# The last stage of a fused attention and mixture-of-experts kernel: the dense part written into PSUM by ScalarE, a fifth place for results, an earlier exponential and earlier stores

## The reference

```python
xn = layernorm(x) * ln_gamma + ln_beta
abel_out = gelu(xn @ abel_w + abel_b)                 # the dense (shared) part
topw, topi = top_k(xn @ moe_gate_w + moe_gate_b, 2)   # two experts per row
w_dense = one_hot(topi) weighted with softmax(topw)
eo = gelu(xn @ ew1[e] + eb1[e]) @ ew2[e] + eb2[e]
moe_out = sum over the two chosen e of w_dense[e] * eo   # then three rotations
gate = sigmoid(concat(abel_out, moe_out) @ gc_w + gc_b)
mixed = abel_out * (1 - gate) + moe_out * gate
return residual + mixed
```

## Time and profile before

| | |
|---|---|
| median of three runs | 1321.17 us |
| the profiled execution | 1317.45 us, span 1315.8 us |
| PE busy in the span | 1175.7 us (89%) |
| DVE busy | 863.6 us (66%) |
| ACT busy | 494.9 us (38%) |
| POOL busy | 417.5 us (32%) |
| mean granted clock of TensorE | 0.935 |
| last expert tile out of PSUM (line 1461) | ends at 1274.80 us |

### The profile page before, as it was taken

The page is one execution under the profiler, slowest core; times in us unless marked ns, Lnnn a source line. Parts: engine busy times, 40 slices in busy tenths (PEclk is TensorE's granted clock), DMA queues, the critical chain, the costliest instruction groups (busy, mean ns, idle before and its releaser), DMA issues.

```text
span 1315.8 us, 25930 instructions
## 1 busy us (share of the span) xinstructions
PE 1175.7 (89%) x7208; PEld 1017.0 (77%) x7209; DVE 863.6 (66%) x2771; ACT 494.9 (38%) x961; POOL 417.5 (32%) x496
## 2 busy tenths in 40 slices
PE   6989969886999999967999989999776999999988
PEld 6746657675888898956889878888664888988977
DVE  7669767745666666677776677676544766666666
ACT  1115624342444344432333333343333344444445
POOL 3003016862444444430000000114562344444430
PEclk9999968777999999988999989999867999999999
DMA  9402324444444533351101110001226633443358
GB/s 297 140 8 97 128 80 153 159 147 157 122 137 136 168 88 95 91 190 49 49 3 47 49 49 1 1 13 53 97 92 235 197 123 122 132 147 107 104 187 284
DMA packets 72688, 149.15 MB, mean 113 GB/s; under 512 B 10950, under 2 KB 36754, under 8 KB 72602
## 3 DMA queue, kind: packets, MB, share of 16 engines
q1 hardware_dynamic: 52234, 93.40, 20.3%
q0 software_dynamic: 19584, 53.92, 13.4%
q10 hardware_dynamic: 784, 0.79, 0.2%
HBM read 82.63 MB, written 65.44 MB: 113 GB/s over the span
## 4 chain that ended last, share of the span: by engine, by line
PE 51%; issue 11%; DVE 6%; POOL 5%; DMA 4%; another core or an unknown queue 3%; ACT 3%; SPq 2%; POOLq 1%; DVEq 0%; ACTq 0%
PE bank L2450 17%; PE bank L1986 7%; PE bank L1987 6%; PE bank L1988 6%; PE bank L2015 3%; DMA xh<-slots_in 3%; PE bank L2068 3%; PE bank L1846 2%; PE bank L2508 2%; POOL slots_in L1562 2%; PE bank L1998 2%; POOL xh L1573 2%; POOLq L1572 1%; PE bank L2461 1%
## 5 line engine op out<-in xcount | busy, mean ns | idle before, releaser
L1986 PE MATMUL bank<-ew,rows 128*128 x852 | 298.9, 351 | 7.4 <-DVE rows L1440 5.2
L1987 PE MATMUL bank<-low_in,rows 128*128 x852 | 274.2, 322 | 0.0
L1988 PE MATMUL bank<-ew,rows 128*128 x852 | 272.8, 320 | 0.0
L1585 POOL DMA_INDIRECT results<-xh x142 | 142.0, 1000 | 292.6 <-DVE xh L1468 272.0
L1986 PEld LDWEIGHTS bank<-ew,rows 128*128 128x128 f32 x852 | 162.0, 190 | 19.0 <-issue 11.8
L1988 PEld LDWEIGHTS bank<-ew,rows 128*128 128x128 f32 x852 | 161.5, 190 | 11.7
L1813 ACT ACTIVATE xh<-bank 128x512 f32<-128x512 f32 x142 | 85.1, 599 | 222.7 <-PE bank L1988 222.7
L1987 PEld LDWEIGHTS bank<-low_in,rows 128*128 128x128 f32 x852 | 162.4, 191 | 6.2
L1477 DVE TENSOR_TENSOR rows<-bank,rows 128x512 fp32r<-128x512 f32 x142 | 98.2, 691 | 95.1 <-ACT rows L202 86.2
L735 POOL TENSOR_TENSOR work<-work,mhalf 128x8 f32<-128x8 f32 x24 | 40.0, 1666 | 298.4 <-DVE work L728 286.1
L1846 PE MATMUL bank<-abw,work 128*128 128x8 f32 (+1 forms) x512 | 113.3, 370 | 18.7 <-ACT work L207 9.3
(11 more groups left out here) (371 smaller groups left out, 2037.1 us busy)
## 6 DMA issues: line engine op xcount, KB each, us to landing
xh<-slots_in POOLq DMA_DIRECT2D x138, 129.0 KB
low_in<-low SPq DMA_DIRECT2D x32, 512.0 KB
ew<-results SPq DMA_DIRECT2D x7, 1032.0 KB, 9.1
xh<-results SPq DMA_DIRECT2D x6, 1032.0 KB, 5.3
dense<-ab SPq DMA_DIRECT2D x12, 512.0 KB
xs<-in_L_attn_a_x_dram SPq DMA_DIRECT2D x4, 1024.0 KB, 8.0
ew<-in_L_ffn_ew_dram SPq DMA_DIRECT2D x2, 2048.0 KB, 13.2
ew<-in_L_ffn_ew_dram SPq DMA_DIRECT2D x4, 1024.0 KB, 14.6
```

The source lines that it names most:

```text
L1585: pool.indirect_dma_start(out=yg, out_offset=bass.IndirectOffsetOnAxis(ap=back[j % RING], axis=0), in_=yr[j % RING], in_offset=None).then_ ...
L1986: pe.matmul(o, hi, f32r(high(c)), start=(c == 0), stop=False)
L1987: pe.matmul(o, hi, f32r(low(c)), start=False, stop=False)
L1988: last = pe.matmul(o, lo, f32r(high(c)), start=False, stop=(stop and c == chunks[-1]))
```

## The change

Four things, all in the last stage of `mixture(1)`:

- The dense part's product leaves TensorE. ScalarE writes share times dense tile, 256 columns, into the PSUM place (`mixed`), and TensorE adds two products to what is there (`start=False`). So that TensorE adds and does not overwrite, it first writes all eight banks once with a matmul that starts a sum (eight of 512 columns, bf16, after the last expert tile); ScalarE waits for these before its first copy. Diagonals are now 6 a group, and the wait for a free bank moves from TensorE to ScalarE.
- Results get a fifth place, in the tile `rows`. Group 4 is loaded right behind `returned(3)`; group g from 5 on waits for group g - 5.
- ScalarE issues the exponential of group g + 1 inside group g, behind the copy of the third tile and ahead of that tile's two diagonals.
- SyncE stores group 0 before it refills for group 7, and the store of group 7 is two halves.

```diff
-            dg = [dg.take(3 * BYP, P) for _ in range(2)]
+            dg = [dg.take(2 * BYP, P) for _ in range(2)]
...
-                        ] + [ew1[:].rearrange("p a e h -> p a (e h)")[:, :, 0:2 * 2 * CW]]
+                        ] + [ew1[:].rearrange("p a e h -> p a (e h)")[:, :, 0:2 * 2 * CW],
+                             rows[:].rearrange("p a b n -> p (a b n)")[:, 0:GT * 2 * CW].rearrange("p (t x) -> p t x", x=2 * CW)]
+            PLACES = len(res_flat)
+            res_place = lambda g: g if g < PLACES else g - PLACES
...
+            def mixed(g, t):
+                return bank[:, 2 * (g % RING) + t // HALF, t % HALF * C:(t % HALF + 1) * C]
+
+            def dense_row(g, t):
+                return ab[:, g * GT + t, :]
...
                 returned(LOWS - 1)
+                if r == 1:
+                    results_in(RING)
...
-                for g in range(RING, NG) if r == 1 else ():
-                    sp.wait_ge(mix_ps, 2 * (g - RING + 1))
-                    sp.wait_ge(last_ok, 3 * (g - RING + 1))
-                    results_in(g)
...
+                    def refill(g):
+                        sp.wait_ge(mix_ps, 2 * (g - PLACES + 1))
+                        sp.wait_ge(last_ok, 3 * (g - PLACES + 1))
+                        results_in(g)
+
+                    def store(some):
+                        sp.dma_start(o[:, some, :], xs[:, some, :]).then_inc(o_st, 16)
+
+                    for g in range(PLACES, NG - 1):
+                        refill(g)
                     for g in range(NG):
+                        if g == NG - 1:
+                            sp.wait_ge(x2_ok, 2 * g + 1)
+                            store(slice(g * GT, g * GT + HALF))
                         sp.wait_ge(x2_ok, 2 * (g + 1))
                         sp.wait_ge(last_ok, 3 * (g + 1))
-                        sp.dma_start(o[:, tiles(g), :], xs[:, tiles(g), :]).then_inc(o_st, 16)
-                    sp.wait_ge(o_st, 16 * NG)
+                        store(tiles(g) if g < NG - 1 else slice(g * GT + HALF, (g + 1) * GT))
+                        if g == 0:
+                            refill(NG - 1)
+                    sp.wait_ge(o_st, 16 * (NG + 1))
...
-                for g in range(NG) if r == 1 else ():
+
+                def raise_gate(g):
                     act.wait_ge(z_ok, g + 1)
                     act.activation(z[g % 2], z[g % 2], ACT.Exp, scale=-1.0).then_inc(ez_ok, 1)
+
+                if r == 1:
+                    raise_gate(0)
+                for g in range(NG) if r == 1 else ():
                     act.wait_ge(gate_ok, 2 * (g + 1))
                     for t in range(BYP):
                         after(act, mix_ps, 2 * (g - 2) + t // HALF + 1)
-                        parts = (gw2[g % 2][:, t, 0:1], gw2[g % 2][:, t, 1:2], shut[g % 2][:, t:t + 1])
-                        for k, part in enumerate(parts):
-                            last = copy(act, dg[g % 2][:, 3 * t + k, :], ident[:], part)
+                        if g == 0 and t == 0:
+                            act.wait_ge(dn_ps, out_past + SLOTS + 1)
+                        if t % HALF == 0:
+                            after(act, x2_ok, 2 * (g - RING) + t // HALF + 1)
+                        copy(act, mixed(g, t), dense_row(g, t), shut[g % 2][:, t:t + 1])
+                        if t == BYP - 1 and g + 1 < NG:
+                            raise_gate(g + 1)
+                        for k in range(2):
+                            last = copy(act, dg[g % 2][:, 2 * t + k, :], ident[:], gw2[g % 2][:, t, k:k + 1])
                         if t % HALF == HALF - 1 or t == BYP - 1:
                             last.then_inc(dg_ok, 1)
...
+                if r == 1:
+
+
+                    pe.wait_ge(y_ok, past + SLOTS)
+                    for b in range(2 * RING):
+                        last = pe.matmul(bank[:, b, :], onesb[0:2 * QROW + E, :], sel[:, 0:BANK // P, :].rearrange("p e c -> p (e c)"),
+                                         start=True, stop=True)
+                    last.then_inc(dn_ps, 1)
...
                         if t % HALF == 0:
                             pe.wait_ge(dg_ok, 2 * g + t // HALF + 1)
-                            after(pe, x2_ok, 2 * (g - RING) + t // HALF + 1)
-                        o = bank[:, 2 * (g % RING) + t // HALF, t % HALF * C:(t % HALF + 1) * C]
-                        src = (result_row(g, t, 0), result_row(g, t, 1), ab[:, g * GT + t, :])
-                        for k in range(3):
-                            last = pe.matmul(o, dg[g % 2][:, 3 * t + k, :], src[k], start=(k == 0), stop=(k == 2))
+                        for k in range(2):
+                            last = pe.matmul(mixed(g, t), dg[g % 2][:, 2 * t + k, :], result_row(g, t, k), start=False, stop=(k == 1),
+                                             skip_group_check=True)
```

More of the change, by code:

```diff
@@ L1089, in mixture @@
             BYP = GT - 1
-            dg = Arena(work[:, T - 2 * 3 * BYP * P:T])
-            assert rt.at <= T - 2 * 3 * BYP * P
-            dg = [dg.take(3 * BYP, P) for _ in range(2)]
+            dg = Arena(work[:, T - 2 * 2 * BYP * P:T])
+            assert rt.at <= T - 2 * 2 * BYP * P
+            dg = [dg.take(2 * BYP, P) for _ in range(2)]
             ntile, tincl, ends = rt.take(E), rt.take(E), rt.take(E)
@@ L1128, in mixture @@
             res_flat = [ew2[:].rearrange("p a e c -> p a (e c)")[:, :, q * 2 * CW:(q + 1) * 2 * CW] for q in range(RING - 1)
-                        ] + [ew1[:].rearrange("p a e h -> p a (e h)")[:, :, 0:2 * 2 * CW]]
+                        ] + [ew1[:].rearrange("p a e h -> p a (e h)")[:, :, 0:2 * 2 * CW],
+                             rows[:].rearrange("p a b n -> p (a b n)")[:, 0:GT * 2 * CW].rearrange("p (t x) -> p t x", x=2 * CW)]
+            PLACES = len(res_flat)
+            res_place = lambda g: g if g < PLACES else g - PLACES
             res = [v.rearrange("p a (t k c) -> p a t k c", k=2, c=CW) for v in res_flat]
+            def mixed(g, t):
+                return bank[:, 2 * (g % RING) + t // HALF, t % HALF * C:(t % HALF + 1) * C]
+            def dense_row(g, t):
+                return ab[:, g * GT + t, :]
             def result_row(g, t, k):
-                v = res[g % RING]
+                v = res[res_place(g)]
                 return v[:, t // v.shape[2], t % v.shape[2], k, 0:C]
@@ L1176, in mixture @@
             if r == 1:
-                y_ld = [(spilled[k], BACK + 32, 16 if k < RING - 1 else 32) for k in range(RING)]
+                y_ld = [(spilled[k], BACK + 32, 16 if k < RING - 1 else 32) for k in range(RING)] + [(s("fifth_results"), 0, 16)]
                 z_ok, ez_ok, gate_ok, x2_ok, o_st = s("z"), s("ez"), s("gate"), s("x2"), s("stored")
@@ L1520, in vector @@
                     if g < NG:
-                        y_loaded, before, one = y_ld[g % RING]
-                        v.wait_ge(y_loaded, before + one * (g // RING + 1))
-                        gates = res[g % RING][:, :, :, :, C]
+                        y_loaded, before, one = y_ld[res_place(g)]
+                        v.wait_ge(y_loaded, before + one * (g // PLACES + 1))
+                        gates = res[res_place(g)][:, :, :, :, C]
                         by_row = lambda w: w.rearrange("p (a t) k -> p a t k", a=gates.shape[1])
@@ L1698, in results_in @@
                 def results_in(g):
-                    v = res_flat[g % RING]
+                    v = res_flat[res_place(g)]
                     if v.shape[1] == GT:
-                        sp.dma_start(v, y[:, tiles(g), :]).then_inc(y_ld[g % RING][0], 16)
+                        sp.dma_start(v, y[:, tiles(g), :]).then_inc(y_ld[res_place(g)][0], 16)
                     else:
@@ L1704, in results_in @@
                             t = g * GT + a * HALF
-                            sp.dma_start(v[:, a].rearrange("p (t x) -> p t x", x=2 * CW), y[:, t:t + HALF, :]).then_inc(y_ld[g % RING][0], 16)
+                            sp.dma_start(v[:, a].rearrange("p (t x) -> p t x", x=2 * CW), y[:, t:t + HALF, :]).then_inc(y_ld[res_place(g)][0], 16)
                 for g in range(LOWS - 1):
```

## The result

The changed kernel took 1316.86 us (median of 7 runs, 1311.61 to 1320.24), the kernel before 1323.32 (7 runs beside it, 1318.21 to 1331.46). The ratio is 0.9948, 95% interval 0.9928 to 0.9969. The profiled execution took 1314.84 us with a span of 1313.2, against 1317.45 and 1315.8.

A forecast was written before the change was run, and what follows sets the result against it. TensorE's 144 records bound the last stage, VectorE and the queue close behind. Group 7's earlier start (1.95), the stretch to TensorE's end (2.50) and the tail (0.5) sum to 4.95 us, from median 1321.17 to 1316.2; own range 1314.5 to 1318.

The forecast's parts named there:

- TensorE leaves the pace: Last stage: TensorE falls from 3.89 to 2.59 us a group, below VectorE's 3.44, so it no longer sets the pace.
- Group 7 begins 1.95 us earlier: VectorE's start of the last group: 1300.07 in place of 1302.02, four groups of 3.44 us after group 3.
- From there to TensorE's end 2.50 less: From group 7's start to TensorE's last record: 7.42 us in place of 9.92.
- The tail, 0.5: End behind TensorE: halving the last store saves 0.5 us, bounds 0 and 0.9.
- ScalarE's copy into PSUM, 0.40: Each 256-column copy of the dense part costs ScalarE 0.40 us, between 0.28 and 0.49.
- Signs of being wrong: Group 3 starting after 1288, a copy into PSUM slower than 0.5, or granted clock below 1 after 1284.
- The starting matmuls, hidden: Eight matmuls before the last stage: ScalarE at worst 0.85 us late, hidden by group 3's wait; cost taken as 0.
- The early exponential: ScalarE's loop with it is 3.3 us against VectorE's 3.44, so issuing it early costs and brings nothing.
- The fifth place: Group 4's results load early, there at 1288.9 and wanted at 1289.75; from group 3 on VectorE waits for nothing.
- The queue's: Rival: shared transfers delay group 3 by up to 2.7 us, giving 1318.9, or hold up group 7's load; chance 0.15.
- TensorE's work: Rival: VectorE's 3.44 us is no floor, so all 10.4 us of removed records return, giving 1310.8; chance 0.09.
- The clock's case: Rival: TensorE's rests lower its clock to 1.2 GHz, 5.2 us a group, giving 1329; chance 0.06.

The follow-up runs named there:

- x3: Changed kernel with all refills ahead of the first store and the last store whole, as before; last stage 37.23 us.
- x2: Changed kernel with the exponential issued at the head of its group, as before; last stage 38.32 us.
- x7: Changed kernel with a semaphore count of its own for group 3's results; 1272.46 us, ratio 0.9940 to the kernel before, last stage 36.15 us.
- x1: Changed kernel with four places for results in place of five; last stage 38.61 us.
- x8: Changed kernel without the stores of groups 0 to 5, which are missing from the output; last stage 36.80 us.
- x4: Changed kernel with the dense part back on TensorE and no starting matmuls; last stage 40.42 us.
- x5: Kernel before with only the dense part moved to ScalarE: four places, late exponential, old stores; last stage 40.56 us.
- x9: Changed kernel without the third term of VectorE's last-tile sum, so its output is incomplete; last stage 36.14 us.
- x10: Kernel before, unchanged, profiled again on the third chip; last stage 42.06 us.
- x6: Changed kernel, unchanged, timed again on the second chip; 1276.81 us, ratio 0.9957 to the kernel before, last stage 36.69 us.

## Why the prediction was right

It forecast 1316.2 us and 0.38% less, from a sum of 4.95 us; 1316.86 and 0.52% less were measured, and 0.40% less by the stage. The sum holds; that the time came out within 0.7 us is in part luck. The prediction started from a median of 1321.17, and the kernel before had 1323.32 in the runs beside the result; from there the same sum gives 1318.4.

- *TensorE leaves the pace.* Right. Twelve records in 2.86 us (2.75 forecast), at full clock, with pauses of 0.49.
- *Group 7 begins 1.95 us earlier.* Measured 2.18 from the start of the stage. Group 3 started no earlier (12.06 against 11.93), as forecast, and the distance of the groups was 3.35 in place of 3.44: the next group's first operation begins 0.08 before the last addition has ended, which a wait had hidden in the earlier trace rows.
- *From there to TensorE's end 2.50 less.* 9.92 became 1307.04 + 2.86 - 1302.37 = 7.53: 2.39 less.
- *The tail, 0.5.* Measured 0.55, and x3 gives it back when undone.
- *ScalarE's copy into PSUM, 0.40.* Measured 0.40 to 0.42.
- *Signs of being wrong.* Two of them came by the letter: group 3 started at 1288.97, after 1288, and the granted clock was 0.50 in the microsecond from 1284 and 0.81 in the next. Both limits were times from the span's start, and the whole stage began 2.53 us later than before. From the start of the stage group 3 came at 12.06, where 1288 would be 13.62, and the clock was back at 1.00 in the microsecond from 1286, where 1284 would be 1286.53.
- *The first store about 12 us earlier.* From the start of the stage 12.37 us in place of 23.02, so 10.65 earlier; nothing in the sum rested on it.
- *The starting matmuls, hidden.* They ran from 1277.39 to 1279.29, 1.90 us, and ScalarE's first copy began at 1279.53, directly behind the first gate. The cover was not even needed.
- *The early exponential "costs and brings nothing here": wrong.* The sum was made with it in place, so its number held, but the sentence compared ScalarE's loop with the early exponential to VectorE's and never to the loop without it. That one is 3.88 us a group, as slow as TensorE was. With the exponential left in its old place the same working would have given the same 4.95, and it would have been 2.0 us too much (x2).
- *The fifth place.* The prediction let no group wait behind group 3, and none did. It gave the fifth load 0.85 us of slack; x7 shows 0.5 to 0.95. What it left open was what the lack of the place would cost, 2.3 us (x1), which I then guessed too low.
- *Rivals.* The queue's did not come: group 3 was not later than the scatter of its start (11.93 to 12.81 in all runs but x7), and x8 rules out that stores held up the loads. TensorE's work did not come back whole: 10.4 us went, 5.1 came back. The clock's case did not come: 1.00 in every microsecond from 1286 to TensorE's end at 1309.90, with pauses up to 1.23 us. So that clock did not swing up and down with the short pauses, which the Trainium skill's "TensorE: Matmul & The Clock Gate", section "A second HAM failure mode: psum-queue depth-cycling", tells of in another kernel.

The first comparison of medians is 1.3 us above the stage's difference, the second 0.8 below it. Neither is outside its interval, and I take both for scatter of the part ahead. That part's length lay between 1271.47 and 1277.38 us in the profiles x1 to x4, on one chip, and between 1231.44 and 1241.20 in x5 to x8, on another. What makes it scatter was not tried.

## What to carry to other kernels

When one engine's run of work is taken off the chain, write down the loops of the others as they will be, in the order of their queues, and compare each part of the change against the loop without it; here four loops (TensorE 3.89 us a group, ScalarE 3.88 with the late exponential, VectorE 3.35, ScalarE 3.29 with the early one) lay so close that ScalarE's part alone gave 0.9 to 1.5 us and the three other parts 1.0 to 1.6, where all together gave 5.1. A place for data that no one misses while the slow engine is slow can be needed as much as the work's removal once it isn't. Where the program scatters by more than the change can bring, measure the stage from an event inside it, not the whole.

## What the runs showed of the hardware that was not expected

- TensorE's clock was at its lower level (0.50 granted, 1.2 GHz) from 1282 us, although the engine had worked until 1279.29 and had rested only 2.4 us. It was still 0.98 in the microsecond from 1281, in which the engine began again, so it fell just behind the restart. In the kernel before it had rested 5.1 us and was at the lower level too. The starting matmuls did not keep it up. Later pauses of 0.5 us in 3.35, and one of 1.23, left it at 1.00.
- The last stage of the kernel before scatters with that clock: 5.00 and 4.38 us for the same twelve records behind the same rest of 5.07 us, which is 0.62 of the 0.64 us between its two profiles.
- The kernel before took 1323.32 us in the runs of the first result, and 1281.16 and 1284.16 on the chips of x5 to x8 and of x9 and x10. In the last stage they hardly differ (42.06 and 41.42); the difference lies ahead of it. GpSimd's idle time before its fetches of line 1573, put down to nothing that the profile shows, was 36.4 us in the first profile of the kernel before and 13.9 in x10; in the kernel after, where this is line 1582, 35.4 and 11.1 (x6). Whether this is the cause was not tried.
